# One core of a graph network: the general path judged inside the last strip, and a normalisation moved to ScalarE

## The reference, cut to what matters

```python
h = jnp.maximum(_layernorm(x), 0.0)              # phase 1 of the kernel
# gcn_conv(h, W, b), twice, relu between:
#   h = h @ W;  out[dst] += h[src] * dinv[src] * dinv[dst]  (self loops too);  + b
x = x + gcn_conv(relu(gcn_conv(h, W1, b1)), W2, b2)
h = jnp.maximum(_layernorm(x), 0.0)              # phase 3 of the kernel
# msg = relu(concat(h[src], edge_attr) @ W1 + b1);  agg = mean of msg by dst
x = x + relu(concat(h, agg) @ W2 + b2)
```

## Time and profile before

| | |
|---|---|
| median of 3 runs (lowest, highest) | 2491.26 us (2489.32, 2493.92) |
| profiled execution, its own time | 2496.99 us |
| its span, first to last instruction | 2494.8 us |
| mean granted TensorE clock | 0.946 of 2.4 GHz |
| busy: TensorE products, weight loads | 2175.6 us (87%), 1787.8 us (72%) |
| busy: VectorE, ScalarE, GpSimd | 1886.4 (76%), 1219.0 (49%), 1824.0 us (73%) |
| last product of the last strip to ScalarE's first instruction of the second phase | 957.1 to 967.7 us |
| third node phase, first turn back to last row | 1295.7 to 1359.3 us |

### The profile page before, as it was taken

How to read it: one execution, slowest core, us unless ns; L and a number is a source line. 1 busy time by engine, 2 the same in 40 slices (tenths; PEclk the granted TensorE clock), 3 DMA queues, 4 the chain that set the end, 5 groups by cost and what they waited for, 6 DMA issues and landing times.

```text
span 2494.8 us, 47576 instructions
## 1 busy us (share of the span) xinstructions
PE 2175.6 (87%) x15568; PEld 1787.8 (72%) x15569; DVE 1886.4 (76%) x3609; ACT 1219.0 (49%) x3297; POOL 1824.0 (73%) x1687
## 2 busy tenths in 40 slices
PE   0355799999999996899985899999999999999996
PEld 0133689997668995788874677877877877787785
DVE  6999999998889884544447677776777777777776
ACT  5845246665667773555543343433433443444440
POOL 0858777888888877777777777777777776777770
PEclk9666999999999998999997899999999999999998
DMA  9414133343333432688873334334343433434332
GB/s 365 162 41 160 48 125 125 133 156 118 135 136 125 183 128 61 231 306 323 308 263 87 105 117 136 108 117 124 101 127 115 127 109 102 136 101 128 115 91 61
DMA packets 127167, 357.85 MB, mean 143 GB/s; under 512 B 34082, under 2 KB 77831, under 8 KB 117687
## 3 DMA queue, kind: packets, MB, share of 16 engines
q10 hardware_dynamic: 24752, 186.56, 19.8%
q0 software_dynamic: 56880, 85.25, 13.1%
q1 hardware_dynamic: 45369, 84.00, 9.8%
HBM read 229.75 MB, written 125.93 MB: 143 GB/s over the span
## 4 chain that ended last, share of the span: by engine, by line
PE 67%; DVE 15%; DMA 5%; issue 4%; POOL 4%; ACT 4%; DVEq 1%; ACTq 0%; POOLq 0%; SPq 0%
PE ps_feat L1095 6%; PE ps_sum L1196 6%; PE ps_node L1095 6%; PE ps_node L1110 5%; PE ps_feat L1110 5%; DVE region_c L2071 5%; PE ps_extra L1234 5%; PE ps_node L1218 4%; PE ps_node L1222 4%; DMA rows_or_lows<-block_lows 3%; ACT rows L1310 3%; PE ps_sum L1222 3%; PE ps_feat L1218 3%; PE ps_sum L1218 3%; PE ps_feat L1222 3%
## 5 line engine op out<-in xcount | busy, mean ns | idle before, releaser
L814 POOL DMA_INDIRECT permuted<-rows_or_lows,slot_of_edge x768 | 902.3, 1175 | 234.1 <-issue 150.3
L796 POOL DMA_INDIRECT rows<-table,region_a x800 | 788.1, 985 | 278.9 <-issue 223.6
L2071 DVE TENSOR_TENSOR region_c<-iota_key,region_c 128x1568 bf16<-128x1568 f16 (+1 forms) x327 | 355.5, 1087 | 0.0
L1416 ACT ACTIVATE region_a<-pre_banks 128x392 bf16<-128x392 f32 x392 | 194.9, 499 | 144.9 <-PE pre_banks L1083 136.7
L1095 PE MATMUL ps_node<-region_a,region_b 128*128 128x256 bf16 (+1 forms) x1911 | 261.9, 267 | 0.0
L1095 PE MATMUL ps_feat<-region_a,region_b 128*128 128x256 bf16 x1764 | 251.6, 272 | 0.0
L580 DVE CAST wide_counts<-region_a 128x1024 fp32r<-128x1024 bf16 (+2 forms) x163 | 118.8, 732 | 153.3 <-PE ps_feat L1110 61.5
L1234 PE MATMUL ps_extra<-msg_parts,target_hot 128*128 128x256 f32 x1176 | 222.5, 305 | 3.7 <-DVE msg_parts L2239 3.7
L578 ACT ACTIVATE wide_counts<-region_a 128x1024 fp32r<-128x1024 bf16 x150 | 158.6, 1060 | 119.2 <-PE ps_feat L1110 55.1
L1196 PE MATMUL ps_sum<-onehot,rows 128*128 128x64 f32 x1600 | 209.8, 276 | 0.2 <-issue 0.2
L1196 PEld LDWEIGHTS ps_sum<-onehot,rows 128*128 128x128 f32 x1600 | 205.0, 200 | 5.3 <-issue 4.2
(11 more groups left out here) (314 smaller groups left out, 4780.9 us busy)
## 6 DMA issues: line engine op xcount, KB each, us to landing
counts<-region_a ACTq DMA_DIRECT2D x23, 3136.0 KB
region_a<-counts ACTq DMA_DIRECT2D x11, 3200.0 KB
region_a<-counts ACTq DMA_DIRECT2D x11, 3072.0 KB
rows_or_lows<-block_lows ACTq DMA_DIRECT2D x72, 448.0 KB
permuted<-region_b SPq DMA_DIRECT2D x25, 833.0 KB, 24.1
region_a<-permuted SPq DMA_DIRECT2D x24, 833.0 KB
rows_or_lows<-edge_cols_in POOLq DMA_DIRECT2D x24, 544.0 KB
region_a<-attr_t_in SPq DMA_DIRECT2D x50, 256.0 KB, 2.9
```

The source lines that it names most:

```text
L796: nc.gpsimd.indirect_dma_start(rows[:, s, j * D:(j + 1) * D], None, tables[2], bass.IndirectOffsetOnAxis(ap=message_rows[:, c * TC + j:c * ...
L814: nc.gpsimd.indirect_dma_start(permuted, bass.IndirectOffsetOnAxis(ap=slot_of_edge[:, r * RT + k:r * RT + k + 1], axis=0), edge_rows_of[:, ...
L1416: nc.scalar.activation(counts[strip % 2][:, :, j * W:j * W + W], count_banks[w % BANKS][:, 0:KEYS].rearrange("p (d h) -> p h d", h=SB), AC ...
L2071: v.tensor_tensor(hot_key(u)[:, :, 0:n], iota_key[:, None, 0:n].to_broadcast([P, UNIT // SIDE, n, SIDE]), keys[:, :, None, :].to_broadcast ...
```

## The change

The verdict is split. `found_ahead`, which covers all strips but the last, stands ahead of the add of the last full strip. `set_flag` covers the last strip's sums and ends with the flag; it stands ahead of the last strip's add. TensorE has the flag's two products after 16 of the last strip's 49 blocks, and waits for the flag, reads it and branches after 32; the remaining 17 blocks and VectorE's last add stand in both branches. In the third node phase the normalisation becomes an ACTIVATE of ScalarE with scale `rstd` and bias `minus_mean` = -mean x rstd, which VectorE writes by one small instruction (`scales_of`); ScalarE's order in a group is root of g + 1, rectify g, normalise g + 1, clear g; VectorE adds the bias rows two groups behind instead of one.

```diff
+FOUND_AT, FLAG_AT = 16, 32
@@ TensorE, end of shared(0)
-                    for h in range(SB):
+                    for h in range(FLAG_AT):
+                        if h == FOUND_AT:
+                            pe.wait_ge(flag_ready, 1)
+                            mm(ps_turn[0:1, 0:P], found[:, 0:1], ident, start=True, stop=True).then_inc(flag_ready, 1)
+                            mm(ps_extra[0:1, 0:1], found[:, 3:4], ones[:, 0:1], start=True, stop=True).then_inc(flag_ready, 1)
                         apply((STRIPS - 1) % 2, h, LAST_WIDTH)
@@ TensorE, behind shared(0)
-            pe.wait_ge(flag_ready, 1)
-            mm(ps_turn[0:1, 0:P], found[:, 0:1], ident, start=True, stop=True).then_inc(flag_ready, 1)
-            mm(ps_extra[0:1, 0:1], found[:, 3:4], ones[:, 0:1], start=True, stop=True).then_inc(flag_ready, 1)
+            def last_applied():
+                for h in range(FLAG_AT, SB):
+                    apply((STRIPS - 1) % 2, h, LAST_WIDTH)
+
             pe.wait_ge(flag_ready, 4)
             flagged = pe.value_load(flag[0:1, 0:1], min_val=0, max_val=1)
             with pe.If(flagged > 0):
+                last_applied()
                 full(0)
+            with pe.Else():
+                last_applied()
@@ ScalarE, node_phase(2)
+                def normalise(g):
+                    act.wait_ge(rstd_ready, NG + 2 * g + 2)
+                    if g >= 2:
+                        act.wait_ge(G["turned"], g + NG - 1)
+                    for b in range(GB):
+                        last = nc.scalar.activation(normed[g % 2][:, b], region_b[:, g * GN + b * P:g * GN + (b + 1) * P], ACT.Identity,
+                                                    bias=minus_mean[:, g % 2, b:b + 1], scale=rstd[:, g % 2, b:b + 1])
+                    last.then_inc(G["normed"], 1)
...
                     if n == 2:
                         if g + 1 < NG:
-                            features(g + 1)
+                            std_of(g + 1)
+                        features(g)
+                        if g + 1 < NG:
+                            normalise(g + 1)
                         clear(g)
@@ VectorE, node_phase(2)
-            def normalise(a, n, g):
+            def scales_of(g):
+                m = g + NG
+                dve.wait_ge(G["std"], m + 1)
+                if g >= 2:
+                    dve.wait_ge(G["normed"], m - 1)
+                v.reciprocal(rstd[:, g % 2], std[:, g % 2]).then_inc(rstd_ready, 1)
                 dve.wait_ge(G["moments"], m + 1)
-                v.reciprocal(rstd[:, g % 2], std[:, g % 2]).then_inc(rstd_ready, 1)
-                for b in range(GB):
-                    last = v.tensor_scalar(normed[g % 2][:, b], a[:, g * GN + b * P:g * GN + (b + 1) * P],
-                                           moments[:, g % 2, b, 0:1], rstd[:, g % 2, b:b + 1], ALU.subtract, ALU.mult)
-                last.then_inc(G["normed"], 1)
+                dve.wait_ge(rstd_ready, NG + 2 * g + 1)
+                v.scalar_tensor_tensor(out=minus_mean[:, g % 2], in0=moments[:, g % 2, :, 0], scalar=-1.0, in1=rstd[:, g % 2],
+                                       op0=ALU.mult, op1=ALU.mult).then_inc(rstd_ready, 1)
...
-                    for g in range(NG + 1):
+                    for g in range(NG + 2):
...
-                        if g:
-                            rows_of(g - 1)
+                        if g >= 2:
+                            rows_of(g - 2)
...
-                            normalise(region_b, n, g + 1)
+                            scales_of(g + 1)
@@ VectorE, end of shared(0) and verdict
+                    dve.wait_ge(C["evacuated"], (STRIPS - 1) * SW + BANKS)
+                    found_ahead()
                     add_strip(STRIPS - 2)
-                    add_strip(STRIPS - 1, LAST_WIDTH)
+                    dve.wait_ge(C["evacuated"], NW + BANKS)
+                    set_flag()
...
+            def set_flag():
+                last = row_sums[:, (STRIPS - 1) * SW:NW]
+                v.tensor_reduce(found[:, 1:2], last, AX.X, ALU.max)
+                link(v.tensor_reduce(found[:, 2:3], last, AX.X, ALU.add))
+                v.tensor_tensor(found[:, 0:1], found[:, 0:1], found[:, 1:2], ALU.max)
+                link(v.tensor_tensor(found[:, 3:4], found[:, 3:4], found[:, 2:3], ALU.add))
                 dve.sem_inc(flag_ready, 1)
                 dve.wait_ge(flag_ready, 3)
...
+            def last_added():
+                add_strip(STRIPS - 1, LAST_WIDTH)
+                dve.drain()
...
-            flagged = verdict()
+            flagged = dve.value_load(flag[0:1, 0:1], min_val=0, max_val=1)
             with dve.If(flagged > 0):
+                last_added()
                 full(0)
+            with dve.Else():
+                last_added()
             dve.sem_inc(G["sums"], 1)
```

More of the change, by code:

```diff
@@ L352, in build @@
         rstd = sb("rstd", [P, 2, GB])
+        minus_mean = sb("minus_mean", [P, 2, GB])
         eps = sb("eps", [P, 1])
@@ L1376, in node_phase @@
                     std_of(0)
-                if n:
+                    normalise(0)
+                if n == 1:
                     features(0)
-                if n == 1:
                     features(1)
                 for g in range(NG):
-                    if n == 2 and g + 1 < NG:
-                        std_of(g + 1)
                     if n == 2:
                         if g + 1 < NG:
-                            features(g + 1)
+                            std_of(g + 1)
+                        features(g)
+                        if g + 1 < NG:
+                            normalise(g + 1)
                         clear(g)
@@ L1966, in node_phase @@
                     mean_and_variance(region_b, n, 0)
-                    normalise(region_b, n, 0)
-                    for g in range(NG + 1):
+                    scales_of(0)
+                    for g in range(NG + 2):
                         if g + 1 < NG:
@@ L2134, in shared @@
                     add_applied(len(APPLIED) - 1)
-                dve.wait_ge(C["evacuated"], NW + BANKS)
                 dve.drain()
@@ L2147, in full, with found_ahead @@
                 dve.drain()
-            def verdict():
+            def found_ahead():
                 link(v.tensor_scalar(range_over[:, 0], range_over[:, 0], float(RANGE_ROWS), None, ALU.is_ge))
@@ L2154, in verdict @@
                 link(v.tensor_scalar(range_bad[:], range_bad[:], 4 * EXACT, None, ALU.mult))
-                link(v.tensor_reduce(found[:, 0:1], row_sums, AX.X, ALU.max))
+                ahead = row_sums[:, 0:(STRIPS - 1) * SW]
+                link(v.tensor_reduce(found[:, 0:1], ahead, AX.X, ALU.max))
                 link(v.tensor_tensor(found[:, 0:1], found[:, 0:1], range_bad[:], ALU.max))
-                link(v.tensor_reduce(found[:, 1:2], row_sums, AX.X, ALU.add))
+                link(v.tensor_reduce(found[:, 1:2], ahead, AX.X, ALU.add))
                 blocks = TARGETS // P
@@ L2162, in verdict @@
                 link(v.tensor_tensor(found[:, 3:4], found[:, 1:2], found[:, 2:3], ALU.subtract))
+                link(v.tensor_reduce(judged[:, 2:3], chunk_window[:, 1], AX.X, ALU.max))
+            def set_flag():
[4 more added lines that the diff above has]
+                link(v.tensor_tensor(found[:, 3:4], found[:, 3:4], found[:, 2:3], ALU.add))
                 dve.sem_inc(flag_ready, 1)
                 dve.wait_ge(flag_ready, 3)
+                v.tensor_scalar(judged[:, 1:2], ps_extra[0:1, 0:1], 0.0, None, ALU.not_equal)
                 link(v.tensor_reduce(judged[:, 0:1], ps_turn[0:1, 0:P], AX.X, ALU.max))
                 link(v.tensor_scalar(judged[:, 0:1], judged[:, 0:1], EXACT, None, ALU.is_gt))
-                link(v.tensor_scalar(judged[:, 1:2], ps_extra[0:1, 0:1], 0.0, None, ALU.not_equal))
-                link(v.tensor_reduce(judged[:, 2:3], chunk_window[:, 1], AX.X, ALU.max))
                 link(v.tensor_reduce(judged[:, 3:4], judged[:, 0:3], AX.X, ALU.max))
@@ L2171, in verdict @@
                 dve.sem_inc(flag_ready, 1)
-                return dve.value_load(flag[0:1, 0:1], min_val=0, max_val=1)
+            def last_added():
+                add_strip(STRIPS - 1, LAST_WIDTH)
+                dve.drain()
             node_phase(0)
```

5 lines of the change are left out of this document (removed).

## The result

The changed kernel takes 2521.48 us (median of 4 runs, 2519.64 to 2528.42), the kernel before 2492.45 us beside it (4 runs, 2489.32 to 2493.92): ratio 1.0123, 95% interval 1.0101 to 1.0146. It is slower by 29 us where I had forecast no change. The profiled execution has a span of 2526.6 us and an own time of 2528.42.

A forecast was written before the change was run, and what follows sets the result against it. GpSimd's scatter queue was taken to gate the message stage, which then runs at GpSimd's and TensorE's pace. Terms 0 (verdict) + 0 (third phase) - 0.05, with +-3 and +-2, gave 2491.0 us, range 2484.0 to 2496.0.

The forecast's parts named there:

- GpSimd's row gates the start of the message stage: Before the first gather: back-to-back scatters, ending at 1368.8 +-3, set the start; the message table has 8 us of slack.
- Verdict: Edge from the last strip to ScalarE's second phase: 6 us earlier (9 if the branch is free, 2 at high ends).
- Third phase: Third node phase, 13 groups: taken as 4 us earlier, ends 3 us later and 6 us earlier; group 3.4 to 4.1 us.
- Neither reaches the end: Of the two edits' 10 us, 0 reach the end; they become TensorE idle time before the first gathered product.
- The rivals on the queue: GpSimd's scatter queue: normalisations hold it up (14.8 us sooner, chance 0.03), or casts fall worse (8 us later, chance 0.05).
- the lock: Rival: VectorE's 52 normalisations hold up GpSimd, so without them the queue ends 14.8 us sooner, 2476.5; chance 0.03.
- the casts: Rival: second convolution's casts fall worse, 203 scatters' mean from 1.060 to 1.10, queue 8 us later, 2499; chance 0.05.
- Nothing of that stage is changed: Message stage behind 1370: 800 gathers, 1067 us at GpSimd's and TensorE's pace, taken as unchanged.
- the slower ones: Slower rivals: casts fall worse, 2499, chance 0.05; third phase becomes the gate, 2491 + a few, chance 0.02.

The follow-up runs named there:

- experiments 7 and 8: Without the last range's 32 scatters: kernel before (7), 2482.93 us, 0.9977; changed kernel with 32 never-run VectorE instructions ahead of its message loop (8), 2474.41 us, 0.9923.
- Experiment 1: Changed kernel with 32 never-run VectorE instructions ahead of the message loop (loop at place 7): 2493.5 us, ratio to the kernel before 0.9994.
- experiment 2: Kernel before, neither edit in it, with 96 never-run VectorE instructions ahead of the message loop (place 104): 2520.73 us, ratio 1.0101.
- experiment 4: Kernel before with only the third phase's part of the change (loop at place 97, no refetching expected): 2505.06 us, ratio 1.0042.
- experiment 3: Kernel before with only the verdict's part of the change (loop at place 14): 2491.65 us, ratio 0.9985.
- experiments 10 and 12: Two of three casts on ScalarE, never-run VectorE instructions ahead of the loop: kernel before (10, place 8) 2494.0 us, 1.001; changed kernel (12, place 123) 2487.3 us, 0.9987.

## Why the prediction was wrong

- *GpSimd's row gates the start of the message stage*: right. Last scatter 1368.91 (forecast 1368.8 +-3), 0.30 us before each scatter, and experiments 7 and 8 move the gate by shortening the row. In the profiled executions with a full row and the casts as before the first gather came at 1370.0 to 1376.3, so +-3 was a little narrow.
- *Verdict*: the gain was mis-sized by 2 us, for a reason that I had not seen. The chain of the kernel after, 945 to 970 us:

```profile
949.53 2.36 PE ps_node L1097 x48
951.89 0.31 PE ps_turn L1145 x2
952.20 0.03 PE ps_extra L1146 x2
952.23 2.47 PE ps_node L1097 x48
954.70 3.45 issue
958.15 4.96 PE ps_node L1097 x51
...
963.60 0.64 ACT rows L1367
```

  The flag was written at 953.01 + 0.14 (forecast 954.5), the branch cost 3.45 us (forecast 3.0), the two products 0.34 (0.6). But the 51 products behind the branch took 0.097 us each in place of 0.050: the stretches show the granted clock at half, 1.2 GHz, right behind TensorE's stop (columns: us, busy of PE, PEld, DVE, ACT, POOL, then clock, DMA share, GB/s).

```profile
949.00:954.00 5.00, 5.00 (x95) 4.78 (x94) 1.66 (x10) 0.00 (x0) 3.78 (x5) 1.00 0.07 16
958.00:963.00 5.00, 4.85 (x51) 4.71 (x51) 0.00 (x0) 0.00 (x0) 3.82 (x4) 0.50 0.33 116
```

  ScalarE starts at 963.60, 4.1 us sooner than the earlier trace rows and not the 6 that I summed. The branch itself may have the same cause as the stops in the message stage. In 954.7 to 958.2, TensorE's stop, the changed kernel has these packets of instructions, and the kernel before has as many in its own 3.02 us:

```profile
q8 instruction: 1, 0.02, 2.4%
q14 instruction: 2, 0.02, 1.5%
```

  The jump passes over the code of the general path. That it is these fetches which set the 3.45 us is not tested.
- *Third phase*: right within its bounds, better than the value taken. Instructions of the kernel after in order:

```profile
1312.82 0.16 DVE L1906 SCALAR_TENSOR_TENSOR minus_mean<-moments,rstd 128x4 f32<-128x4 f32 x1
...
1313.49 1.64 ACT L1355 ACTIVATE rows<-region_b,minus_mean,rstd 128x128 f32<-128x128 f32 x4
...
1349.15 0.69 DVE L1939 TENSOR_TENSOR region_c<-ps_node,msg_b 128x512 f32<-128x512 f32 x1 [2.66 <-PE ps_node L985]
```

  ScalarE's normalisations take 1.64 us a group, over my "1.24 at most", which I had from the single instruction of another line; the group is now ScalarE's, 3.35 us. The last row is written at 1349.15, 9.5 us sooner than the earlier trace rows, forecast 10 for both edits and 1347 to 1352 for the time. Less the 4.1 us of the verdict that is 5.4 us from the third phase, where I took 4: the one edit gave less than I had summed and the other more, and that their sum came out near 10 is luck.
- *Neither reaches the end*: right. Experiment 1 has 0.9994.
- *The rivals on the queue*: neither came. For the lock, the scatters of the third phase took 960 ns without VectorE's normalisations and 962 with them, and the row did not end 14.8 us sooner. For the casts, the mean went from 1060 to 1066 ns, 1.2 us over 202 scatters.
- *The failed step* is one sentence, "Nothing of that stage is changed", and the term of 0 that it put for the change of the 1067 us of the message stage. It was true of the instructions, their order and their waits, and not of where VectorE's loop lies in its instruction stream. That term measured 32 us in the profiled execution and 29 us in the medians; the place alone takes 28 us of it away (experiment 1) and puts 26 us on the kernel before (experiment 2). No rival named it; the slower ones were about GpSimd's queue and the third phase. The shift of the loop was to be had beforehand, by a count of the VectorE instructions that the diff adds and removes ahead of it; its price was not, as the miss in experiment 4 shows.

## What to carry to other kernels

When a diff adds or removes instructions ahead of a long hardware loop, treat the loop's own time as an open term, even if no line of it is changed, and price it by a twin that has only idle code ahead of it. The sign in a profile is idle time put down to "issue" on one engine, at changing lines but in every pass, together with more packets on that engine's instruction queue; look for it before any theory on data. And before calling an optimization worthless or harmful, measure it with the loop put back in its old place: here the edits by themselves cost nothing and not 29 us, and gained about 9 us as soon as what hid them was shortened.

## What the runs showed of the hardware

- A VectorE loop of 284 listed instructions ran without refetching from five places of its block of 128 and was fetched anew in each pass from five others, about five packets of 8192 bytes at a time. The kernels with it took between 5 and 29 us longer. In 1560 to 1570 us of the changed kernel each packet came with a stop of VectorE of 2.2 to 2.5 us.
- TensorE, at 2.4 GHz in 949 to 954, stood for 3.45 us and ran its next 51 products at 1.2 GHz (0.097 us in place of 0.050). So the stop cost 2.4 us beyond its length. With the verdict alone (experiment 3) it was 3.49 us and the next 48 products took 0.081 us each.
- ScalarE's 128x128 FP32 normalisation with a scale and a bias per row took 0.41 us each back to back, 486 ns as the mean of one over the stage; VectorE's took 361 ns as the mean of one.
- The casts delay the scatters: with 113 in place of 163 on VectorE the scatters beside them took 1.042 us in place of 1.060 (1.044 and 1.036 in experiments 10 and 12), and the row ended 3 to 5 us sooner.
